# Weight-preparation units split into a load part and a compute part, with loads issued two units ahead and the compute parts moved in front of stage D

## The reference

```python
xn = layernorm(x)
k, r = xn @ Wk.T, xn @ Wr.T                 # 1024 x 1024 each, v = r
y = wkv_scan(-exp(time_decay), time_first, k, r)   # recurrence over the 4096 tokens
attn = (sigmoid(r) * y) @ Wo.T
ffn = (silu(xn @ wg.T) * (xn @ wu.T)) @ wd.T   # wg, wu: 3072 x 1024, wd: 1024 x 3072,
                                               # int32 weights times 1/127
out = x + attn + ffn
```

## Time and profile before

| | us |
|---|---|
| runs of the kernel, median of 2 (lowest, highest) | 2046.72 (2041.14, 2052.30) |
| the profiled execution, device time | 2033.59 |
| its span from first to last instruction, slowest core (core 6) | 2031.9 |
| spans of the other cores | 2017.3 to 2029.8 |
| PE busy | 1530.2 (75%) |
| DVE busy | 627.7 (31%) |
| ACT busy | 467.8 (23%) |
| POOL busy | 121.7 (6%) |

### The profile page before, as it was taken

How to read it: one execution, slowest core, us unless ns; L and a number is a source line. 1 busy time by engine, 2 the same in 40 slices (tenths; PEclk the granted TensorE clock), 3 DMA queues, 4 the chain that set the end, 5 groups by cost and what they waited for, 6 DMA issues and landing times.

```text
span 2031.9 us, 24788 instructions; the slowest of 8 cores (2017.3 to 2031.9 us)
## 1 busy us (share of the span) xinstructions
PE 1530.2 (75%) x8089; PEld 804.2 (40%) x8192; DVE 627.7 (31%) x1094; ACT 467.8 (23%) x803; POOL 121.7 (6%) x112
## 2 busy tenths in 40 slices
PE   2655565564564218999998998998998998998995
PEld 2544454454454113433433433433433433433431
DVE  0466767767767101102202202202201201201201
ACT  3334544544545311101101101101200200200200
POOL 1011121121121110000000000000000000000000
PEclk9867787787787558999999999999999999999998
DMA  6323454554454767557558558648638639638641
GB/s 99 79 47 79 109 126 98 119 127 95 113 130 89 139 148 175 133 183 170 134 169 187 142 148 198 152 125 214 158 110 220 165 100 225 156 111 220 153 118 62
DMA packets 573611, 280.59 MB, mean 138 GB/s; under 512 B 477232, under 2 KB 526384, under 8 KB 573488
## 3 DMA queue, kind: packets, MB, share of 16 engines
q1 hardware_dynamic: 557744, 237.05, 45.7%
q0 software_dynamic: 15744, 41.95, 10.4%
HBM read 251.70 MB, written 52.43 MB: 150 GB/s over the span
## 4 chain that ended last, share of the span: by engine, by line
PE 72%; ACT 9%; DVE 6%; issue 6%; DMA 6%; SPq 0%; ACTq 0%; DVEq 0%; POOL 0%; POOLq 0%
PE psA L655 17%; PE psB L666 16%; PE psRb L696 9%; PE psR L451 6%; PE psK L451 6%; PE psB L696 4%; PE psA L696 4%; PE psRb L708 3%; ACT S L535 3%; DMA pp_in<-wd 2%; DVE sttb L388 2%; ACT S L531 2%; ACT xn_fm L433 2%; DVE res L717 1%; PE psB L708 1%
## 5 line engine op out<-in xcount | busy, mean ns | idle before, releaser
L655 PE MATMUL psA<-xnc,wgu 128*128 128x512 bf16 x1505 | 372.1, 389 | 62.5 <-DMA wgu<-wgu_s 30.6
L674 ACT ACTIVATE sil<-psA,cst 128x512 f32<-128x512 f32 x192 | 131.9, 687 | 1035.3 <-PE psA L655 1035.3
L666 PE MATMUL psB<-xnc,wgu 128*128 128x512 bf16 x1504 | 363.1, 382 | 1.9 <-issue 0.2
L679 DVE SCALAR_TENSOR_TENSOR h_sb<-sil,cst,psB 128x512 bf16<-128x512 f32 x192 | 143.6, 748 | 598.3 <-PE psB L666 522.7
L655 PEld LDWEIGHTS psA<-xnc,wgu 128*128 128x128 bf16 x1536 | 152.4, 100 | 250.6 <-issue 77.0
L666 PEld LDWEIGHTS psB<-xnc,wgu 128*128 128x128 bf16 x1536 | 151.5, 99 | 185.6 <-issue 8.0
L696 PE MATMUL psRb<-wdt,h_sb 128*128 128x512 bf16 x752 | 194.3, 377 | 38.6 <-DVE h_sb L679 8.9
L717 DVE TENSOR_TENSOR res<-psRb,x 128x512 f32<-128x512 f32 x32 | 22.1, 692 | 525.9 <-PE psB L708 523.1
L451 PE MATMUL psK<-xn_fm,wkT 128*128 128x256 bf16 x1024 | 150.1, 295 | 3.1 <-ACT xn_fm L433 3.1
L451 PE MATMUL psR<-xn_fm,wrT 128*128 128x256 bf16 x1024 | 148.3, 293 | 5.1 <-DVE S L471 5.1
L696 PEld LDWEIGHTS psRb<-wdt,h_sb 128*128 128x128 bf16 x768 | 61.3, 96 | 171.6 <-issue 125.7
(11 more groups left out here) (58 smaller groups left out, 1077.6 us busy)
## 6 DMA issues: line engine op xcount, KB each, us to landing
wgu<-wgu_s SPq DMA_DIRECT2D x192, 512.0 KB, 4.7
wdt<-wdT_s SPq DMA_DIRECT2D x192, 256.0 KB, 2.7
x_tok<-x SPq DMA_DIRECT2D x16, 1024.0 KB, 5.9
x<-x SPq DMA_DIRECT2D x8, 2048.0 KB, 15.2
out<-res POOLq DMA_DIRECT2D x8, 2048.0 KB, 8.3
wgu_s<-pp_stage SPq DMA_DIRECT2D x48, 256.0 KB, 2.8
xn_s<-xn_fm SPq DMA_DIRECT2D x16, 512.0 KB, 5.7
outp_s<-outb SPq DMA_DIRECT2D x16, 512.0 KB, 5.8
```

Source lines behind the costliest of these rows:

```text
L655: last = e.matmul(psA[pab][:], wgu_t[wsl][:, (iu * CC + cc) * P:(iu * CC + cc + 1) * P], xnc[sl][:, cc * TT2:(cc + 1) * TT2], start=(cc == ...
L666: last = e.matmul(psB[pab][:], wgu_t[wsl][:, (iu * CC + cc) * P:(iu * CC + cc + 1) * P], xnc[sl][:, cc * TT2:(cc + 1) * TT2], start=(cc == ...
L674: lambda e, pab=pab: e.activation(out=sil_b[pab][:], in_=psA[pab][:], func=AF.Silu, scale=cst[:, 3:4]),
L679: lambda e, hc=hc, pab=pab: e.scalar_tensor_tensor(out=h_sb[:, hc * TT2:(hc + 1) * TT2], in0=sil_b[pab][:], scalar=cst[:, 4:5], in1=psB[pa ...
```

## The change

Each unit function no longer records its operations when it is called. It returns two functions, one that records the load (`dma_part`) and one that records transposes, copies and writes (`cmp_part`), and the number of its input buffer. Buffer numbers are the same as before. Three call sites differ:

- Before the loop, the 16 units of Wk and Wr are recorded as: load 0, load 1, compute 0, load 2, compute 1, load 3 and so on.
- Just before the loop at line 570, the loads of the first two units are recorded.
- In the loop, the four compute parts are recorded in front of `stage_d(ch)` and no longer behind it. After each compute part the loads of up to two units ahead are recorded, if the input buffer's last user has been recorded.

```diff
+            startup = [pp_mat_unit(wk_d, cc, wkT, r_wkT) for cc in range(CC)]
+            startup += [pp_mat_unit(wr_d, cc, wrT, r_wrT) for cc in range(CC)]
+            startup[0][0]()
+            startup[1][0]()
+            for i, u in enumerate(startup):
+                u[1]()
+                if i + 2 < len(startup):
+                    startup[i + 2][0]()
...
+            def pp_can_dma(j, cmp_done):
+                sj = pp_get(j)[2]
+                for i in range(j - 1, -1, -1):
+                    if pp_get(i)[2] == sj:
+                        return i < cmp_done
+                return True
+
+            def pp_drip(n_units):
+                nonlocal pp_idx, pp_dma_idx
+                while pp_idx < n_units:
+                    while pp_dma_idx <= pp_idx:
+                        pp_get(pp_dma_idx)[0]()
+                        pp_dma_idx += 1
+                    pp_get(pp_idx)[1]()
+                    pp_idx += 1
+                    while (pp_dma_idx < min(pp_idx + 2, len(pp_units))
+                           and pp_can_dma(pp_dma_idx, pp_idx)):
+                        pp_get(pp_dma_idx)[0]()
+                        pp_dma_idx += 1
...
+            while (pp_dma_idx < min(2, len(pp_units))
+                   and pp_can_dma(pp_dma_idx, pp_idx)):
+                pp_get(pp_dma_idx)[0]()
+                pp_dma_idx += 1
             for ch in range(NC1):
...
                     stage_a_post(ch + 2)
+                pp_drip((len(pp_units) * (ch + 1)) // NC1)
                 stage_d(ch)
-                n_units = (len(pp_units) * (ch + 1)) // NC1
-                while pp_idx < n_units:
-                    pp_units[pp_idx]()
-                    pp_idx += 1
             stage_e(NC1 - 1)
 
-            while pp_idx < len(pp_units):
-                pp_units[pp_idx]()
-                pp_idx += 1
+            pp_drip(len(pp_units))
```

More of the change, by code:

```diff
@@ L303, in pp_wgu_unit @@
                 pp_mat_unit.ctr += 1
+                ssl = pp_mat_unit.ctr % 2
                 src_ap = dram_ap(src_d, hc * P * C, [[C, P], [1, C]])
-                bd.op("gpsimd",
-                      lambda e, sl=sl, src_ap=src_ap: e.dma_start(
-                          out=pp_in[sl][:, 0:C], in_=src_ap),
-                      writes=[r_pp_in[sl]], dma_sem=f"d_pp{sl}")
-                def tr(e, sl=sl):
-                    last = None
-                    for cc in range(CC):
-                        last = e.transpose(psP[sl][:, cc * P:(cc + 1) * P],
-                                           pp_in[sl][:, cc * P:(cc + 1) * P], ident[:])
-                    return last
@@ new lines, in cmp_part, with tr @@
+                def cmp_part(sl=sl, ssl=ssl, hc=hc, iu=iu):
+                    def tr(e, sl=sl):
+                        last = None
+                        for cc in range(CC):
+                            last = e.transpose(psP[sl][:, cc * P:(cc + 1) * P],
+                                               pp_in[sl][:, cc * P:(cc + 1) * P], ident[:])
+                        return last
+                    bd.op("tensor", tr, reads=[r_pp_in[sl], r_ident], writes=[r_psP[sl]])
+                    bd.op("scalar",
+                          lambda e, sl=sl, ssl=ssl: e.copy(pp_stage[ssl][:], psP[sl][:, 0:C]),
+                          reads=[r_psP[sl]], writes=[r_pp_stage[ssl]])
+                    dst = dram_ap(wgu_s, ((hc * 2 + iu) * CC) * P * P,
+                                  [[P, P], [P * P, CC], [1, P]])
+                    bd.op("sync",
+                          lambda e, ssl=ssl, dst=dst: e.dma_start(out=dst, in_=pp_stage[ssl][:]),
+                          reads=[r_pp_stage[ssl]], writes=[r_wgu_s[hc]], dma_sem=f"d_pps{ssl}")
@@ L329, in pp_wd_unit @@
                 pp_mat_unit.ctr += 1
+                ctr = pp_mat_unit.ctr
                 src_ap = dram_ap(wd_d, dc * P * H, [[H, P], [1, H]])
[L331 to L355 removed]
@@ new lines, in dma_part, with cmp_part, tr @@
+                def dma_part(sl=sl, src_ap=src_ap):
+                    bd.op("gpsimd",
+                          lambda e, sl=sl, src_ap=src_ap: e.dma_start(
+                              out=pp_in[sl][:, 0:H], in_=src_ap),
+                          writes=[r_pp_in[sl]], dma_sem=f"d_pp{sl}")
+                def cmp_part(sl=sl, dc=dc, ctr=ctr):
+                    for g in range(3):
+                        psl = (sl + g) % 2
+                        def tr(e, sl=sl, g=g, psl=psl):
+                            last = None
+                            for j in range(CC):
+                                hc = g * CC + j
+                                last = e.transpose(psP[psl][:, j * P:(j + 1) * P],
+                                                   pp_in[sl][:, hc * P:(hc + 1) * P], ident[:])
+                            return last
+                        bd.op("tensor", tr, reads=[r_pp_in[sl], r_ident], writes=[r_psP[psl]])
+                        ssl = (ctr + g) % 2
+                        bd.op("scalar",
+                              lambda e, psl=psl, ssl=ssl: e.copy(pp_stage[ssl][:], psP[psl][:, 0:C]),
+                              reads=[r_psP[psl]], writes=[r_pp_stage[ssl]])
+                        dst = dram_ap(wdT_s, (g * CC) * P * C + dc * P,
+                                      [[C, P], [P * C, CC], [1, P]])
+                        bd.op("sync",
+                              lambda e, ssl=ssl, dst=dst: e.dma_start(out=dst, in_=pp_stage[ssl][:]),
+                              reads=[r_pp_stage[ssl]],
+                              writes=[r_wdT_s[g * CC + j] for j in range(CC)],
+                              dma_sem=f"d_pps{ssl}")
```

87 lines of the change are left out of this document (32 added, 55 removed).

## The result

The changed kernel takes 2107.84 us in the median of its runs, the kernel before 2039.16 beside it. The ratio is **1.0325, 95% interval 1.0289 to 1.0361**: slower by 3.3%. (Executions in which one die ran at a lower granted clock are left out of every ratio here, for both kernels; where too few are left for a ratio, the times are given.) The profiled execution spans 2111.1 us on core 0, its slowest; the cores lie between 2070.9 and 2111.1, with mean granted clocks of 0.873 to 0.883 (0.890 to 0.894 before).

A forecast was written before the change was run, and what follows sets the result against it. One loop of waits through all engines bounds a pass, DVE's share allowing at most 1.7 us gain. Twelve wg/wu passes +60 and the tail +6.6 make +67 on 2040: 2107 us, range 2050 to 2135.

The forecast's parts named there:

- The floor: In each pass, DVE's way to pair 2's psR group (the deciding group) limits any gain to 1.7 us, 20 in all.
- Steps 2 and 3: POOL's loads in a wg/wu pass: PE waits for the third unit's load, B starts at 438.1; next pass's loads follow.
- Step 4: First weight write of a pass (W0), behind a 512 KB write and amid two loads: lands in 6.6 us.
- Step 5: Second weight write (W1) is held on SP until W0 lands, then takes 5.0 us, between 2.8 and 7.0.
- Step 6: Stage D, exps and multiply follow the last copy, so pair 2's psR group (the deciding group) starts 3.4 us later.
- Step 7: PE idles 4.9 us inside B, so two groups run at the lower clock: 1.6 us a pass, between 0 and 2.6.
- (a): Tail: the first wd load is issued in iteration 13, so the second goes out earlier, -7.4 us.
- (b): Tail: stage E's product waits for late D and stands on POOL before the sixth wd load, +2 us (0 to 4.5).
- (c): Tail: stage D of chunk 15, E, product and its write now come behind the last wd copy, +12.0 us.
- R1: Rival: weight writes only queued, not held up by loads, W1 in 2.8; +21, about 2061 us; chance 0.2.
- R2: Rival: the reorder works, W0 and W1 both land in 2.8, group 1.3 early; -9, about 2031 us; chance 0.12.
- R3: Rival: writes held up but no clock loss, 3.4 us a pass; +47, 2087 us; 0.65 together with the forecast.

The follow-up runs named there:

- e9: The changed kernel with four input buffers, loads up to four units ahead, four staging buffers and wg and wu writes apart: ratio 1.0003 to the kernel before.
- e14: The e9 kernel plus 78 transposes nobody reads on PE, between the psK and psR groups of pair 2: ratio 0.9844 to the kernel before.
- e2: The changed kernel with stage D put back in front of the units, loads still issued two units ahead: ratio 1.0027 to the kernel before.
- e1: The kernel before with whole units moved in front of stage D, each load directly before its transposes, nothing prefetched: ratio 1.0295 to the kernel before.
- e4: The changed kernel with four staging buffers in place of two: ratio 1.0033 to the kernel before.
- e3: The changed kernel with wg and wu writes of one row block no longer waiting for each other: ratio 1.0110 to the kernel before.
- e5: The changed kernel with stage D in front of the units again in iterations 14 and 15: ratio 1.0327 to the kernel before.
- e12: The e9 kernel plus 40 transposes nobody reads on PE, between the psK and psR groups of pair 2: ratio 0.9943 to the kernel before.
- e13: The e9 kernel with wd units cut into 24 rounds, their own input buffer, at most two rounds an iteration, 24 filling transposes: ratio 0.9880 to the kernel before.
- e15: The e13 kernel with a pass's loads issued right behind stage E's product, rounds alternating two and one, 44 filling transposes: 1933.27 and 1933.71 us.

## Why the prediction came out

The total was right (2107 forecast, 2107.84 measured). That it is right to the microsecond is luck: the passes cost less than forecast, the tail and the Wo passes more, and the slowest core grew by 68.7 us where the mean grew by 64.8.

| us | forecast | measured, mean of the cores |
|---|---|---|
| wg/wu passes | 12 x 5.0 = 60 | 12 x 4.13 = 49.5 |
| start and Wo passes | 0 | 3.0 + 2.3 = 5.3 |
| tail (wd part) | 6.6 | 10.9 |
| rest | 0 | -0.9 |
| sum | 67 | 64.8 |

**The floor (DVE's way, at most 1.7 a pass).** Right: the deciding group can come 1.6 us earlier and no more (21.74 in e9), and the pass is 35.99 with no waits and the clock kept (e14), against 35.85 from the earlier trace rows. What I had not seen is that the gain could not be had even with all waits gone, because PE then idles 5 us in front of the deciding group (e9).

**The units of Wk, Wr and Wo at 0.** Right for Wk and Wr: e2 has their new start-up and reaches product 1 at 143.4 us (143.9 before). The 5.3 us are the Wo units' (iterations 0 and 1). The 3.0 before product 1 come from the order: e1, with the old start-up, has 3.4. In the pass behind it the order alone costs 2.6 (e1), the early loads alone 1.6 (e2) and both together 2.3. A Wo unit has no staging buffer, so this is not the writes; what it is, no run took apart. The bound that I gave (1.7 each) covers two thirds of it.

**Step 1, copy 0.** Right: it starts when its transposes are through, 3.4 us after s, in place of 10.7.

**Steps 2 and 3, the loads.** PE waits for the third load 6.11 us, as forecast (431.0 to 435.5 plus what it was early). But of the cost of loads I had only a part: these waits alone just use up what DVE's floor would allow (e4 has them and a pass of 37.47), and the loads issued ahead cost 1.3 us a pass more, by way of the writes (after against e1).

**Step 4, W0 in 6.6.** Right: 6.8 is the median of the 88 passes (5.1 to 8.8). The 8.7 us of the pass shown are near the upper end; there W0 is on its way together with two loads and the write of xn, and the second load takes 8.4 where it took 6.1.

**Step 5, the second write waits for the first.** Right in kind, and the largest single cause: without it 3.24 of the 4.13 us are gone (e3). W1 took 4.4 and not 5.0 in the median (4.1 in the pass shown), so step 4 and 5 together are off by 0.4 us. The rule of the Trainium skill (DMA: Bandwidth & Descriptors, "Queues, rings and completion order"), by which a completion waits for earlier writes across an engine's queues, put W1 toward 7.0; W1 took 2.6 to 6.3 us in the 88 passes, below that in all of them. That it takes 1.6 us more than in e1 agrees with the rule, and so does the slow W0, but both would also be so if the transfers merely shared the engines, and no run tells the two apart.

**Step 6, the deciding group +3.4.** +2.8 on the mean (26.15 for 23.31), +4.9 in the slowest core's pass shown. The chain is the one forecast: exposed D, exp, multiply, group; four staging buffers break it (e4).

**Step 7, the clock, 1.6.** It is there: 1.1 us a pass behind the deciding group (15.32 for 14.21), after 3.6 us idle where the forecast had 4.9. In the pass shown, 3.60 us idle, a group at 1.03, and then three at 1.72, 1.92 and 1.23, 1.7 us more. The full 1.6 showed in e9, where PE was 5.00 idle, and its removal in e14. So the two terms that were mis-sized in a pass are this one (1.6 for 1.1) and step 6 (3.4 for 2.8), both too high.

**The tail.** Read on core 0: the end of B (PE), the wd loads and the product (POOL), then SP, ACT and SP again.

```profile
714.10 1.04 PE L496 MATMUL psR<-xn_fm,wrT 128*128 128x256 bf16 x8
...
718.44 0.59 POOL L343 DMA_DIRECT2D pp_in<-wd  x1 [8.45 <-PE psP L354]
...
757.73 0.53 POOL L343 DMA_DIRECT2D pp_in<-wd  x1 [12.03 <-PE psP L354]
768.35 4.50 POOL L597 TENSOR_TENSOR outb<-S 128x2048 bf16<-128x2048 f32 x1 [10.10 <-DVE S L590]
772.79 0.59 POOL L343 DMA_DIRECT2D pp_in<-wd  x1
789.22 0.53 POOL L343 DMA_DIRECT2D pp_in<-wd  x1 [15.83 <-PE psP L354]
801.87 0.53 POOL L343 DMA_DIRECT2D pp_in<-wd  x1 [12.12 <-PE psP L354]
...
772.93 0.36 SPq L603 DMA_DIRECT2D outp_s<-outb  x1
773.44 43.30 SPq L365 DMA_DIRECT2D wdT_s<-pp_stage  x12
...
783.93 1.01 ACT L360 COPY pp_stage<-psP 128x1024 bf16<-128x1024 bf16 x1 [13.31 <-DMA wdT_s<-pp_stage]
...
832.52 0.36 SPq L676 DMA_DIRECT2D xnc<-xn_s  x1
```

and the last wd load of the kernel before (its POOL timeline):

```profile
729.08 0.53 POOL L332 DMA_DIRECT2D pp_in<-wd  x1 [11.96 <-PE psP L341]
```

- (a) The second wd load goes out 718.44 - 715.14 = 3.3 us after B, before 655.00 - 643.77 = 11.2: -7.9, forecast -7.4. It needs the new order too: in e5, which has the early load but D in front again, this load goes out 11.2 us after B.
- (b) From that load to the last it is 83.4 us in place of 74.1: +9.3, forecast +2. The product of stage E ahead of the sixth load makes that step 15.1 us in place of 12.35, the +2.7 that I had. The next step is 16.4, another +4.1, and this I had missed: the write of that product stands on SP too, ahead of the wd writes. Two copies ended by 770.6, but their writes go out only from 773.44 on, behind the one of 772.93 and into the load of 772.79, and the third copy waits 13.31 us for them. The order of a queue was followed on POOL and not on SP. The remaining 2.5 us are spread over the other steps.
- (c) From the last load to the first of phase 2 it is 832.52 - 801.87 = 30.7, before 749.77 - 729.08 = 20.7: +10.0, forecast +12.0. D, E and the product are exposed as forecast; the last write landed in 3.4 us, not 5.2.

Together +11.4 on this core, against +6.6.

**The rivals.** R1 (W1 in 2.8, 38.75 a pass) has its landing times in e1 (7.2 and 2.8), and there the pass is 40.35: the deciding group comes 2.2 late and not 1.2, and the clock costs 0.8. e3 comes near R1's number (38.41), but by another way, two slow writes side by side. R2 needs W1 landed early; e4 is its counterpart, where nobody waits for W1. Its deciding group comes at 23.26 us and not at the 22.1 of R2 (448.5 - 426.44), since the second load lands 7.1 us after its issue (median) and not 6.1, and D starts behind it; the clock is not lost there. So R2 would have been short of its gain even with its own condition met. R3, no loss of clock, is near in number (3.4 forecast, 4.13 measured), but the clock's loss is there.

## What to carry to other kernels

Before work is moved in front of a stage on an engine, look at what that work waits for: here four copies waited for two staging buffers and through them for two writes in turn, and the stage behind them inherited the wait. Loads issued early are only early for their reader; for every small write issued at the same moment they are late, so a place in the loop where no write is on its way can be worth more than the earliest one (35.98 against 41.05 us a pass, with two more edits in between that the rows above speak against). A wait that is taken away in front of a series of matmuls can come back as a lower clock: the idle stretch must be filled or be kept outside the part that is in series.

## What the runs showed of the hardware

A write of 256 KB from SP landed in 2.8 us (median, kernel before). In the kernel after it took 6.8 with two weight loads and a write of 512 KB on their way (W0) and 4.4 with the next two loads issued around it (W1; 2.8 without them in e1). With four loads issued within 4 us around the writes the median was 12.1 to 12.7 (e9, e12, e13, e14), and 4.2 with the same four loads moved away (e15).

An idle stretch of PE of 5.00 us before the deciding group cost two groups at 1.87 and 1.85 (the 1.2 GHz level) in place of 1.04; 2.77 us of idle time behind 2.40 us of transposes cost parts of three groups; 2.01 and 0.97 us around 4.52 us of transposes cost none. In the kernel after, 3.6 us (mean) in front of pair 2 cost 1.1 us a pass. In e9 most groups of B on cores 4 to 7 took 1.22 us, and 1.04 on cores 0 to 3; no run takes apart why.
